# Layer norms on a Trainium2 core: GpSimd subtracts the mean instead of adding a negated copy of it

## The reference

```python
def _layernorm(x, axis=-1, eps=1e-05):
    m = jnp.mean(x, axis=axis, keepdims=True)
    v = jnp.var(x, axis=axis, keepdims=True)
    return (x - m) / jnp.sqrt(v + eps)

    h = _layernorm(x, axis=-1) * (1 + ca) + sa
    x = x + ga * _L0_attn_ref(h, ...)      # causal attention, one head
    h = _layernorm(x, axis=-1) * (1 + cb) + sb
    x = x + gb * _L0_ffn_ref(h, ...)       # 8 experts, the top one for each row
    h = _layernorm(x, axis=-1) * (1 + ca) + sa
    x = x + ga * _L1_attn_ref(h, ...)      # 16 heads of 8 channels, full attention
    h = _layernorm(x, axis=-1) * (1 + cb) + sb
    x = x + gb * _L1_ffn_ref(h, ...)       # two linear layers of each batch's own
```

## Time and profile before

| | |
|---|---|
| median of 3 executions | 1775.31 us (1772.64, 1775.31, 1781.6) |
| the profiled execution | 1772.89 us, its span 1771.6 us |
| PE busy | 1668.0 us, 94% |
| DVE busy | 1499.3 us, 85% |
| ACT busy | 1378.6 us, 78% |
| POOL busy | 733.7 us, 41%, 1195 instructions |
| clock granted to TensorE | 0.988 of full speed |

### The profile page before, as it was taken

How to read it: one execution, slowest core, us unless ns; L and a number is a source line. 1 busy time by engine, 2 the same in 40 slices (tenths; PEclk the granted TensorE clock), 3 DMA queues, 4 the chain that set the end, 5 groups by cost and what they waited for, 6 DMA issues and landing times.

```text
span 1771.6 us, 54921 instructions
## 1 busy us (share of the span) xinstructions
PE 1668.0 (94%) x23327; PEld 658.5 (37%) x23337; DVE 1499.3 (85%) x2257; ACT 1378.6 (78%) x1934; POOL 733.7 (41%) x1195
## 2 busy tenths in 40 slices
PE   5777999999999999999999999999999999999998
PEld 3543433334333343334333343333433343222224
DVE  4669888898889988899888988899888998999973
ACT  4443779887798778887798878987788877887885
POOL 2321345526543465434564365434664355112110
PEclk9998999999999999999999999999999999999999
DMA  2131111122210322112210213103211122201111
GB/s 71 50 122 33 39 56 53 33 63 59 84 59 23 91 71 69 35 37 74 83 56 27 73 48 94 49 24 96 63 59 36 38 73 71 70 24 50 35 28 35
DMA packets 97234, 99.96 MB, mean 56 GB/s; under 512 B 11117, under 2 KB 81437, under 8 KB 96989
## 3 DMA queue, kind: packets, MB, share of 16 engines
q1 hardware_dynamic: 96188, 95.66, 18.1%
q10 hardware_dynamic: 800, 0.79, 0.1%
HBM read 61.02 MB, written 34.57 MB: 54 GB/s over the span
## 4 chain that ended last, share of the span: by engine, by line
PE 67%; DVE 15%; ACT 13%; issue 3%; DMA 1%; POOL 1%; ACTq 0%; SPq 0%; DVEq 0%; POOLq 0%
PE pv_psum L818 23%; PE side_psum L551 15%; PE buffer L802 12%; PE buffer L792 10%; DVE row_max L1329 9%; ACT p L1028 7%; PE side_psum L641 2%; PE side_psum L608 2%; PE buffer L551 1%; ACT o_sb L1037 1%; DVE s L1177 1%; ACT s L946 1%; DVE st_f L1087 1%; ACT s L939 1%; ACT hT_b L1017 1%
## 5 line engine op out<-in xcount | busy, mean ns | idle before, releaser
L1329 DVE TENSOR_REDUCE row_max<-buffer 128x2 f32<-128x1024 f32 x1024 | 1235.3, 1219 | 163.6 <-PE buffer L792 151.0
L1028 ACT ACTIVATE p<-buffer 128x1024 f32<-128x1024 f32 x1024 | 1048.2, 1025 | 209.1 <-PE buffer L802 193.3
L818 PE MATMUL pv_psum<-p,v 128*9 128x256 f32 x8192 | 583.8, 381 | 5.8 <-ACT o_sb L1037 5.2
L792 PE MATMUL buffer<-k_ops,q_ops 48*128 48x512 bf16 x2048 | 396.1, 384 | 17.8 <-ACT p L1028 7.7
L802 PE MATMUL buffer<-q_ops,k_ops 51*128 51x512 bf16 x2048 | 400.5, 388 | 6.7 <-DVE row_max L1329 5.2
L818 PEld LDWEIGHTS pv_psum<-p,v 128*9 128x9 f32 x8192 | 149.7, 89 | 316.8 <-issue 234.0
L802 PEld LDWEIGHTS buffer<-q_ops,k_ops 51*128 51x128 bf16 x2048 | 98.1, 92 | 371.7 <-issue 237.2
L1462 POOL TENSOR_TENSOR hm<-masks,hT_f 128x1024 f32<-128x1024 bf16 x56 | 120.4, 2150 | 107.5 <-PE side_psum L551 107.5
L792 PEld LDWEIGHTS buffer<-k_ops,q_ops 48*128 48x128 bf16 x2048 | 99.4, 94 | 116.5 <-ACT p L1028 98.7
L1477 POOL TENSOR_SCALAR nm_parts<-nm 128x16 bf16<-128x16 f32 x64 | 16.3, 255 | 268.2 <-DVE nm L1254 267.8
L551 PE MATMUL side_psum<-we,hm 128*32 128x128 f32 x3648 | 121.1, 274 | 0.0
(11 more groups left out here) (296 smaller groups left out, 1654.8 us busy)
## 6 DMA issues: line engine op xcount, KB each, us to landing
masks<-masks_rows SPq DMA_DIRECT2D x16, 1024.0 KB, 6.5
q_ops<-products SPq DMA_DIRECT2D x128, 96.0 KB
k_ops<-products SPq DMA_DIRECT2D x128, 96.0 KB
products<-q_parts SPq DMA_DIRECT2D x16, 384.0 KB, 2.6
products<-k_parts SPq DMA_DIRECT2D x14, 384.0 KB, 2.8
attention<-o_sb SPq DMA_DIRECT2D x248, 18.0 KB
x<-in_L_attn_inputs SPq DMA_DIRECT2D x8, 512.0 KB, 4.3
products<-q_parts SPq DMA_DIRECT2D x16, 256.0 KB, 3.0
```

What stands on the lines that cost most here:

```text
L792: m = e.matmul(buffer[:, hh, :], q_ops[rows_of(hh, K_MAX), slot, of, i * P:(i + 1) * P], k_ops[rows_of(hh, K_MAX), slot, of, halves(half)[ ...
L818: m = e.matmul(pv_psum[q:q + VW, half * QUARTER:(half + 1) * QUARTER], v1[b % 2][:, kb, 2 * hp + hh, :], p_sb[n % KEPT][:, hh, part * QUAR ...
L1028: e.activation(p_sb[n % KEPT][:, :, :], unit("exp", n)[0][:, :, :], ACT.Exp).then_inc(S["exp_done"], 1)
L1329: e.tensor_reduce(mx[pair % 2][:, :, i, half], unit("max", n)[0][:, :, :], axis=AX.X, op=ALU.max).then_inc(S["max_done"], 1)
```

## The change

GpSimd no longer makes minus the mean. `norm_small` is two instructions, and both forms of `norm_apply` read the mean itself from `mv` and subtract it. The numbers are the same. `sm[:, 0]` is not used any more, and `mv` is read later than before, until the rows are normalised. No wait is added, and no transfer is touched. In the changed file the lines of GpSimd's program behind the removed one stand one lower: variance plus epsilon is L1357, the power L1358, the application L1364.

```diff
-        def norm_apply(src, xn, sm, half, small, signal):
+        def norm_apply(src, xn, mv, sm, half, small, signal):
             dve.wait_ge(*small)
             tiles = halves(half)[0]
             for t in range(tiles.start, tiles.stop):
-                m = e.tensor_scalar(xn[:, t, :], src[:, t, :], sm[:, 0, t:t + 1], sm[:, 2, t:t + 1], ALU.add, ALU.mult)
+                m = e.tensor_scalar(xn[:, t, :], src[:, t, :], mv[:, t, 0:1], sm[:, 2, t:t + 1], ALU.subtract, ALU.mult)
             m.then_inc(signal, 1)
...
         def norm_small(mv, sm, half, signal):
             tiles = halves(half)[0]
-            e.tensor_scalar(sm[:, 0, tiles], mv[:, tiles, 0], -1.0, 0.0, ALU.mult, ALU.add)
             after(e.tensor_scalar(sm[:, 1, tiles], mv[:, tiles, 1], 1.0, EPS, ALU.mult, ALU.add))
             e.tensor_tensor(sm[:, 2, tiles], sm[:, 1, tiles], minus_half[:, tiles], op=ALU.pow).then_inc(signal, 1)
 
-        def norm_apply(src, xn, sm, half, small, signal):
+        def norm_apply(src, xn, mv, sm, half, small, signal):
             pool.wait_ge(*small)
             tiles = halves(half)[0]
             for t in range(tiles.start, tiles.stop):
-                m = e.tensor_scalar(xn[:, t, :], src[:, t, :], sm[:, 0, t:t + 1], sm[:, 2, t:t + 1], ALU.add, ALU.mult)
+                m = e.tensor_scalar(xn[:, t, :], src[:, t, :], mv[:, t, 0:1], sm[:, 2, t:t + 1], ALU.subtract, ALU.mult)
             m.then_inc(signal, 1)
```

More of the change, by code:

```diff
@@ L1115, in apply @@
                 dve.wait_ge(S[f"x2_{half}"], 1)
-            xn, sm = (xn_f, sm_f) if which else (xn_attn, sm_attn)
-            norm_apply(xs[0], xn, sm, half, norm("small", b, which, half), norm("xn", b, which, half)[0])
+            xn, mv, sm = (xn_f, mv_f, sm_f) if which else (xn_attn, mv_attn, sm_attn)
+            norm_apply(xs[0], xn, mv, sm, half, norm("small", b, which, half), norm("xn", b, which, half)[0])
         for half, part in ((0, 0), (0, 1), (1, 0), (1, 1)):
@@ L1312, in apply_b @@
             dve.wait_ge(S["side_filled"], side["channels_b", b - 1, half].filled)
-            norm_apply(xs[b % 4], xn_b, sm_b, half, (S["small_b"], 2 * b + half + 1), S["xn_b"])
+            norm_apply(xs[b % 4], xn_b, mv_b, sm_b, half, (S["small_b"], 2 * b + half + 1), S["xn_b"])
         def ffn(b, half):
@@ L1385, in apply @@
                 pool.wait_ge(S[f"x2_{half}"], b + 1)
-            xn, sm = (xn_f, sm_f) if which else (xn_attn, sm_attn)
-            norm_apply(xs[b % 4], xn, sm, half, norm("small", b, which, half), norm("xn", b, which, half)[0])
+            xn, mv, sm = (xn_f, mv_f, sm_f) if which else (xn_attn, mv_attn, sm_attn)
+            norm_apply(xs[b % 4], xn, mv, sm, half, norm("small", b, which, half), norm("xn", b, which, half)[0])
         stats(0, 0, 0, 1)
```

## The result

The changed kernel takes 1798.64 us (median of 4 runs, 1797.63 to 1800.95), the kernel before, on the same chip, 1774.31 us (1772.64 to 1781.6). The ratio is 1.014, with a 95% interval of 1.012 to 1.016: slower by 24 us. The forecast was 1773.2 us, no change, with a range up to 1781.

A forecast was written before the change was run, and what follows sets the result against it. TensorE, busy 94% of the span, holds 67% of the chain; GpSimd counts only where engines wait for a norm's small numbers. Terms -0.22 - 0.26 - 0.26 - 0.12 = -0.86, so 1774.1 - 0.9 = 1773.2 us, range 1766 to 1781.

The forecast's parts named there:

- The removed instruction: 64 GpSimd instructions in norm_small: each call ends up to 0.26 us earlier, relieving GpSimd of 16.6 us, nearly all off-path.
- Place by place: Gains where the chain meets norm_small: -0.22, -0.26, -0.26 in batch 0, -0.12 in batch 7, 0 elsewhere; sum -0.86 us.
- The first item, norm 1 half 0: Batch 0, norm 1, half 0: VectorE's 0.22 us idle before the application would be saved, -0.22 us.
- Rival 1, the port: Batch 0, norm 1: the earlier power holds up VectorE's L1177 through the shared port; +0.3 us, 1774.4; chance 0.15.
- The changed instruction: The application, 256 times on GpSimd and VectorE: subtracting with a scalar from mv takes 454 ns, as addition; 658 for a rival.
- Rival 2, the slower subtraction: GpSimd applications at 658 ns: norms end 0.56 us later at norm 2, half 1, in 7 batches; +3.2 us, 1777.3; chance 0.10.
- To pass 0.5% the same way, one application would have to take over 0.8 us: Limit stated for a slower GpSimd subtraction: a loss beyond 0.5% needs over 0.8 us, more than any row that size shows.
- The sign test: Forecast wrong if sections between 125 and 1650 us change length by over 1 us, or an application changes its duration.

The follow-up runs named there:

- forms: Kernel before plus 39 GpSimd instructions, 13 kinds of two-step operation, three times each; medians with memory scalars: (mult, add) 447 ns, (mult, subtract) 802; no total time given.

## Why the prediction was wrong

- **The removed instruction**: right. 0.28 us from the first small instruction to the power, 1131 instructions; alone it leaves 720.2 us of GpSimd's work (721 predicted) and changes nothing that can be measured.
- **Place by place**: mostly right. VectorE's idle time at batch 0, norm 2 fell from 1.23 to 1.00 us and from 1.69 to 1.43 (0.97 and 1.43 predicted). The first item, norm 1 half 0, kept its 0.22 us: the power again starts only when L1175 is done.
- **Rival 1, the port**: it did not happen. L1177 at 48.74 us took 1.09 us again. Its premise failed: the small addition started at 48.13 us, 0.04 us behind L1175 and not ahead of it, and was held up beside it once more, for 0.62 us; the power started at 48.84, behind L1177, and took 1.86 us as before. What L1177 does behind a power that started first, no run here shows. Rows 12 were no test of it either: those four applications read one tensor each, L1177 reads two.
- **The changed instruction**: here the prediction failed. It took 454 ns "since subtraction is addition's sibling", and kept 658 ns, the farthest row, for a rival. Both ends were wrong: measured are 792 ns, above the two. The row of the comparison differs from the application in two things, the operation and where the scalars come from, and only the first was seen. 658 ns is the price with two immediates; two scalars from memory add 140 to 150 (forms). Addition with its 454 ns had them, so nothing in rows 13 allowed 658 to be taken as the upper end.
- **Rival 2, the slower subtraction**: the mechanism was right, with a chance of 0.10, and the size was not: +3.2 us against +24. By its own formula, with a group measured at 1.38 us more, a norm ends 1.12 us later; in 7 batches that gives 7.8 us, and place B shows 7.7. Missing are place A (14.0) and place C (5.3). The rival counted the margin of the rows that an application writes, one group at a time. Even at 658 ns place A would have had two groups ahead of it, 2 x 0.82 - 2 x 0.26 = 1.12 us against a margin of 0.85.
- **"To pass 0.5% the same way, one application would have to take over 0.8 us"**: it took 0.79, and the loss is 1.4%, for the same reason. The half clock, 4.3 us, was in no case.
- **The sign test**: "the forecast is wrong if an application changes its duration". It did. The stretch from 125 to 1650 us, which was to keep its length to within 1 us, holds the places A, B and C.

What stays open: why the clock falls behind the wait in batches 1, 2 and 5 and not in 3, 4 and 6, whether another order of GpSimd's queue would help if it left no gap, and why addition with addition is slow where multiplication with multiplication is not. No kernel run here beats the kernel before.

## What to carry to other kernels

An operation swapped for its sibling is a new instruction: take its price from a row that has the same pair of operations and the same kind of scalars, or leave the price open, upwards too. For what a slower instruction costs, sum its extra time over all of its kind from the engine's last idle time to each consumer, and hold that against the consumer's margin, for those that are queued behind it as well; an engine at 41% of the span can be at 94% in the stretch that counts. Before work is moved within such a stretch, look at what it fills: here it had filled the wait for the statistics, and moving it left GpSimd idle for 2.09 us and made the next consumer late. Less work in the stretch took most of the wait away.

## What the runs showed of the hardware

- GpSimd, 128x128 f32, one tensor and two scalars from memory: 442 to 454 ns (one median of three at 492) for add with mult in either order and for mult with mult, 792 to 879 ns for every other pair tried; with immediates 292 to 298 and 645 to 658. VectorE takes 340 ns for addition and subtraction alike. The Trainium skill (GPSIMD Engine Reference, Engine selection) calls one-input work on GpSimd "roughly line-rate", in a row on add, mul and max. Beside VectorE's 340 ns for the norms' application, GpSimd takes 1.3 times that for the addition, 2.3 times for the subtraction and 2.4 times for (max, mult), so it holds here for the first alone.
- In the changed kernel the granted clock fell to 1.2 GHz right behind TensorE's waits of 1.47 us in three places out of six; it cost 1.4 to 1.5 us each time, as much again as the wait. The four transposes took 1.07 us there in batch 1 and 0.63 in batch 3.
